# Attention loop of a two-layer decoder: copies moved between and ahead of exponentials, two sums moved ahead of pieces

## The chip, the cores and the metric

The program runs on one core of a Trainium2 chip. The time is the device time of one execution in microseconds (us). Five engines of the core work side by side, each through its own instructions in order, and wait for each other by semaphores: PE (TensorE, matmuls and transposes), ACT (ScalarE), DVE (VectorE), POOL (GpSimd) and SP, which here issues transfers. A matmul writes to `ps`, eight banks of PSUM of 128 x 512 words; only ACT, DVE and PE touch those here, so most results of PE have to be copied out by ACT or DVE before PE may use the bank again.

## The reference

Two decoder layers over x (2 x 512 x 128, that is 1,024 tokens) with a context of 2 x 77 rows. Each layer adds self attention, cross attention and a routed feed-forward block to x, each on a layer norm of x. The change lies in one loop, which holds the second layer's self attention, and beside it the first part of its cross attention:

```python
def _L1_attn_ref(x, w_q, w_k, w_v, w_o):          # 16 heads of 64
    scores = jnp.einsum('bhsq,bhtq->bhst', q, k)
    masked = jnp.where(causal, -jnp.inf, scores)
    weights = jax.nn.softmax(masked / jnp.sqrt(jnp.float32(dq)), axis=-1)
    out = jnp.einsum('bhst,bhtv->bhsv', weights, v)
    ...
    return jnp.einsum('bsf,df->bsd', cat, w_o)

def _L1_xattn_ref(x, knowledge_embeddings, ...):  # 16 heads of 8, 77 keys
    scores = jnp.einsum('bhsd,bhnd->bhsn', Q, K) / SCALE
    topk_scores, topk_indices = jax.lax.top_k(scores, 32)
    sparse_weights = jax.nn.softmax(topk_scores, axis=-1)
    context = jnp.einsum('bhsk,bhskd->bhsd', sparse_weights, sel_V)
    return context @ Wo.T + bo
```

The 32 largest of 77 scores are found on DVE in four rounds of eight: `max` gives the eight largest of a row, `match_replace` strikes them out.

## The kernel before

**Units.** The self attention is cut by pairs of heads (8) and by stages of 256 queries (4), which gives 32 values of j. A j is one unit U where the queries see few keys (stages 0 and 2: one unit holds a block of 128 keys and one of 256), or two units (stages 1 and 3: 384 keys, then 512). There are 48 units: 0 to 7 are stage 0, 8 to 23 stage 1, 24 to 31 stage 2, 32 to 47 stage 3. `FIRST[j]` is the first unit of j, `STAGE[k]` the first of a stage.

**What one unit goes through.** PE makes the scores (`scores(U)`, two heads, with the causal mask as a matmul), DVE takes the row maxima (`row_max`, L1164), ACT the exponentials with their sums (`exps`, L1608: two instructions for each block, one for each head, so four in a unit of two blocks), DVE the reciprocals (`row_inv`, L1170), POOL multiplies (`divide`, L712), PE turns the weights (`turn`, L2274), ACT copies the turned weights out (`evac_pt`, L1621, tile `prT`), and PE sums the values (`values(j)`, matmuls on `prT`) into bank 6. `evac_cat(j)` (L1616, the 128 x 256 copies into `sel_mem`, where `catT` lies) copies that sum out. Bank 6 is shared: before PE may project the values of the next heads (`project_v`, matmuls on `wT_hi` and `xt_hi`) or sum the next j, that copy has to be done (`cat_ready`).

**The loop.** `for U in range(NU)` stands once for each engine, and its body's order is the engine's order. In step U, PE does scores(U + 2), projects queries and keys (`project_qk`, bank 4) or values for a later j, turns U, and sums the j that ended with unit U - 1 (the sum stands ahead of the turn in the units of `VALUES_FIRST`). The second half of `turn(U)` writes bank 4 and so waits until ACT has copied the newly projected queries and keys (`evac_qk`, L1592). ACT in step U copies out what is due (`evac_cat`, `evac_qk`, `evac_v`), then `evac_pt(U)`, then `exps(U + 2)`, then the rest. DVE does `row_max(U + 2)`, `row_inv(U + 1)`, and a piece of the cross attention.

**Pieces.** From unit 12 to 46 the loop carries pieces (n, r): group n of four heads, round r of the four rounds of eight. One round is `eight` and `remove` on DVE (L1209 and L1219, eight instructions each, the latter with eight short loads). From n = 4 on, a unit with r = 2 does rounds 2 and 3. POOL follows with `shift`, `gone` and `pick`; PE turns the picked weights of n in two halves (`weights_x`, L2336), ACT copies each half out (`weights_T`, L1669, 77 x 512 into `sel_mem`), PE multiplies by the values (16 matmuls of nine columns, `context`), ACT copies that (`evac_cx`, L1663). All of these use bank 7 in turn, and PE's list `seven` holds what has to be done with the bank before it is written again.

**Ends of stages.** When a stage's heads are summed, PE projects them (`project_out`), DVE adds the product to x and takes the statistics of the next norm (`add_attention`), POOL makes the inverse deviation (`rstd_two`, L720, and the offset, L722), ACT applies the norm (`apply_two`, L1635), PE turns the result (`norm_two`, L2310). The same follows the cross attention of stages 0 and 1: at unit 36 and 44 (`OUT`) DVE normalises the context (`context_norm`, L1235), PE turns and projects it (`project_context`, matmuls on `w_x1T` and `cnT`), and in the next unit DVE adds it to x (`add_context`, L1244), after which come the statistics (L1174 to L1181). The projected context lies in bank 6, and PE waits for that sum to x before the next `values`.

Of the kernel before, what the change touches and what calls it, by code (L numbers as in the profile page):

```python
# [17 lines left out]
B, S, D, P = 2, 512, 128, 128  # L18
# [5 lines left out]
NP = H // 2  # L24
# [9 lines left out]
FIRST, UNIT, STAGE = [], [], []  # L34
# [9 lines left out]
NU = len(UNIT)  # L44
STAGE.append(NU)
FIRST.append(NU)
OUT = (36, 44)
# [15 lines left out]
def piece_of(U):  # L63

    if 12 <= U < 28:
        return divmod(U - 12, 4)
    if 29 <= U < 47:
        return 4 + (U - 29) // 3, (U - 29) % 3
    return None, None


NS = 2 * TB + E - 1
BIG = 4096.0

# [36 lines left out]
def decoder(nc, x_in, ctx_in, a0_wq, a0_bq, a0_wk, a0_bk, a0_wv, a0_bv, x0_wq, x0_bq, x0_wk, x0_bk, x0_wv,  # L111
# [5 lines left out]
    with ExitStack() as held:  # L117
# [732 lines left out]
        def _(dve):  # L850
# [375 lines left out]
            def context_norm(k):  # L1226

                dve.wait_ge(cx_ready, 4 * (k + 1))
                all_of = cx[:, k % 2, :, :].rearrange("p n (t h d) -> p n t h d", t=2, h=4)
                dve.reciprocal(cinv[:, :, :].rearrange("p n a -> p (n a)"),  # L1230
                               cx[:, k % 2, :, :].rearrange("p n (a d) -> p (n a) d", d=DX + 1)[:, :, DX])\
                   .then_inc(dve_step, own.up())
                dve.wait_ge(dve_step, own.now())
                for t in range(2):
                    dve.tensor_tensor(cn[:, t, :].rearrange("p (n h d) -> p n h d", h=4, d=DX),  # L1235
                                      all_of[:, :, t, :, 0:DX],
                                      cinv[:, :, 4 * t:4 * t + 4].unsqueeze(3).to_broadcast([P, 4, 4, DX]),
                                      ALU.mult).then_inc(cn_ready, 1)

            def add_context(k, source):  # L1240
                dve.wait_ge(xo_ps, k + 1)
                dve.wait_ge(bias_added, k + 1)
                t = slice(2 * k, 2 * k + 2)
                dve.tensor_tensor(x[:, t, :], x[:, t, :], source.rearrange("p (t d) -> p t d", t=2), ALU.add)\  # L1244
                   .then_inc(xo_used, 1)
                dve.wait_ge(xo_used, k + 1)
                stats_two(k, gn_var)

# [3 lines left out]
            for U in range(NU):  # L1252
                n, r = piece_of(U)
                if U + 2 < NU:
                    row_max(U + 2)
                if U + 1 < NU - 1:
                    row_inv(U + 1)
                for k in range(2):
                    if U == OUT[k]:
                        context_norm(k)  # L1260
                if r is not None:
                    eight(n, r)
                    remove(n, r)
                if double_step(U):
                    eight(n, 3)
                    remove(n, 3)
                if U == 0:
                    apply_first(1)
                if U == 2:
                    norm_stats(7)  # L1270
                if U == 3:
                    norm_apply(7, 9)
                for k in range(3):
                    if U == STAGE[k + 1] + 1:
                        add_attention(k, ps[:, (6, 7, 6)[k], 0:2 * P])
                if U == NU - 3:
                    row_inv(NU - 1)
                for k in range(2):
                    if U == OUT[k] + 1:
                        add_context(k, ps[:, 6, 0:2 * P])  # L1280


            def gates(i, first, n, bank):
# [135 lines left out]
            for j in range(NS):  # L1419
                gate(j)  # L1420
                if j == 4:
                    context_norm(2)
                if j == 6:
                    add_context(2, ps[:, 4, 0:2 * P])
                if j == 11:
                    gates(1, 4, 2, 4)
                if j == 13:
                    shares_of(1, 4, 2)
                if j == 14:
                    chosen_of(1, 4, 2)  # L1430
                cross(E + j)
            for i in range(4 * E):
                gate(NS + i)
                if i % 2 == 0 and i:
                    combine(i // 2 - 1)
                if i == 5:
                    context_norm(3)
                if i == 7:
                    add_context(3, ps[:, 4, 0:2 * P])
                if i == 12:  # L1440
                    gates(2, 6, 2, 4)
                if i == 14:
                    shares_of(2, 6, 2)
                if i == 15:
                    chosen_of(2, 6, 2)
                if i in (14, 15):
                    add_sparse(i - 14)
                cross(E + NS + i)
# [4 lines left out]
        def _(act):  # L1453
# [144 lines left out]
                act.activation(v_all[:, 2 * h:2 * h + 2, g:g + 2, :].rearrange("p t g n -> p t (g n)"),  # L1598
                               ps[:, bank, :].rearrange("p (t n) -> p t n", t=2), ACT.Copy).then_inc(v_ready, 1)

            def exps(U):
                s = U % 2
                act.wait_ge(nmax_ready, through(U))
                if U >= 3:
                    act.wait_ge(pt_ps, U - 2)
                for c, at, i in UNIT[U][1]:
                    for h in range(2):
                        act.activation(pr[U % 3][:, h, at:at + (c + 1) * P], ps[:, 2 * s + h, at:at + (c + 1) * P],  # L1608
                                       ACT.Exp, bias=nmax[:, i % 8, h:h + 1], accum_out=rsum[:, i % 8, h:h + 1])\
                           .then_inc(ex_ready, 1)  # L1610
# [21 lines left out]
            def apply_two(k, rstd_done, ready):  # L1632
                act.wait_ge(rstd_done, k + 1)
                for t in (2 * k, 2 * k + 1):
                    act.activation(xn[:, t, :], x[:, t, :], ACT.Identity, bias=offset[:, t:t + 1], scale=rstd[:, t:t + 1])\  # L1635
                       .then_inc(ready, 1)
# [49 lines left out]
            for U in range(NU):  # L1686
                n, r = piece_of(U)
                spare = ps[:, 7, 0:2 * P]
                for j in range(4 * NP - 1):
                    if U == FIRST[j + 1] + 1:  # L1690
                        evac_cat(j)
                for j in range(3, 4 * NP):
                    if U == FIRST[j] - 3:
                        evac_qk(j, 4)
                        if j in (NP + 2, 2 * NP + 2):
                            tokens_high(j // NP + 1)
                for j in range(2, 4 * NP, 2):
                    if U == FIRST[j] - 1:
                        evac_v(j, 6)
                for k in range(3):  # L1700
                    if U == STAGE[k + 1] + 3:
                        evac_qc(k, spare)
                if U == 12:
                    scores(0, 1, 7)
                if U == 13:
                    scores(1, 1, 7)
                if U == 28:
                    scores(4, 0, 7)
                if r == 0 and n + 1 in EARLY:
                    scores(n + 1, 0, 7)  # L1710
                if r == 2 and n >= 1:
                    weights_T(n - 1, 1, 7)
                evac_pt(U)
                if U == NU - 3:
                    weights_T(n - 1, 0, 7)
                if U + 2 < NU:
                    exps(U + 2)
                for k in range(3):
                    if U == STAGE[k + 1] + 2:
                        apply_two(k, qn_rstd, qn_ready)  # L1720
                for k in range(2):
                    if U == OUT[k] + 2:
                        apply_two(k, gn_rstd, gn_ready)
                if U == 1:
                    tokens_both(1, 8, spare)
                if U == 4:
                    norm_T(7, 9)
                if U == 11:
                    scores(0, 0, 7)
                if U == 12:  # L1730
                    scores(1, 0, 7)
                if U == 28:
                    scores(4, 1, 7)
                if r == 0 and n + 1 in EARLY:
                    scores(n + 1, 1, 7)
                if r == 1 and n >= 1 and U != NU - 3:
                    weights_T(n - 1, 0, 7)
                if r == 2 and n >= 1:
                    evac_cx(n - 1, 7)
                if r == 2:  # L1740
                    weights_x(n)
                for k in range(3):
                    if U == STAGE[k + 1] + 2:
                        norm_two(k, qnT_ps, qnT_ready, spare)
                for k in range(2):
                    if U == OUT[k]:
                        evac_cn(k, spare)
                    if U == OUT[k] + 3:
                        norm_two(k, gnT_ps, gnT_ready, ps[:, 6, 0:2 * P])
# [985 lines left out]
```

## Time and profile before

| What | Value |
|---|---|
| median of 3 runs (lowest to highest) | 580.23 us (576.71 to 580.39) |
| the profiled execution: its time, its span | 578.94 us, 577.1 us |
| busy, share of the span: PE, DVE, ACT, POOL | 89%, 67%, 54%, 39% |
| the chain that ended last, by engine | PE 58%, DVE 19%, ACT 11%, issue 5%, POOL 5% |
| mean granted clock of TensorE | 0.991 |

The loop fills the span from about 132 us (the scores of unit 0) to 388 us. The median is 0.2% over the profiled execution's time, and sums below are made against 578.94 us. In rows of the trace a time stands first (us from the span's start), then how long the instruction or a run of like instructions took; what stands in brackets is how long the engine was idle just before, and who ended that. Matmuls and transposes are pipelined, so those of a run overlap.

### The profile page before, as it was taken

To read this page: it belongs to the slowest core of one execution; us is meant where nothing else is said; L and a number is where in the kernel's file an instruction comes from. 1 tells how busy PE (TensorE), PEld (TensorE's weight loads), DVE (VectorE), ACT (ScalarE), POOL (GpSimd) and SP (SyncE) were. 2 spreads that over 40 slices of the span, in tenths; PEclk is the share of its full clock that TensorE was granted. 3 is DMA by queue.
4 is the path that set the end of the run, shared out by engine and by line. 5 is a ranking of instruction groups with operands and counts; after the bars stand their busy time and mean duration, and the time that the engine had idled before them with its cause. 6 is when DMAs were issued, how large, how long until landed. Compare 5 with 4: busy or idle time off the path is not lost.

```text
span 577.1 us, 12108 instructions
## 1 busy us (share of the span) xinstructions
PE 513.5 (89%) x3929; PEld 408.6 (71%) x3929; DVE 387.7 (67%) x2194; ACT 311.0 (54%) x779; POOL 224.8 (39%) x236
## 2 busy tenths in 40 slices
PE   4888779998998999988999889988889899899997
PEld 2566347866766677767677657677668779799997
DVE  3576775634422697775498799988968889544633
ACT  2343325436786677674875557657765464232221
POOL 5014950004434464562554556634832443340000
PEclk9999999999999999999999999999899999999999
DMA  4700105704000000000000000005400000010000
GB/s 117 214 1 15 46 25 148 205 15 165 2 0 1 2 2 2 1 2 1 2 2 2 1 2 1 2 2 165 136 26 20 15 15 20 10 33 2 28 1 10
DMA packets 24089, 21.04 MB, mean 36 GB/s; under 512 B 2175, under 2 KB 18643, under 8 KB 24027
## 3 DMA queue, kind: packets, MB, share of 16 engines
q1 hardware_dynamic: 23515, 19.21, 11.2%
q0 software_dynamic: 512, 1.05, 0.6%
q8 instruction: 33, 0.54, 0.4%
q14 instruction: 29, 0.24, 0.1%
HBM read 17.22 MB, written 3.03 MB: 35 GB/s over the span
## 4 chain that ended last, share of the span: by engine, by line
PE 58%; DVE 19%; ACT 11%; issue 5%; POOL 5%; DMA 1%; DVEq 0%; ACTq 0%; POOLq 0%
PE ps L1880 48%; PE ps L2274 5%; DVE wk L1219 3%; ACT w_mem L1608 3%; DVE top L1209 2%; DVE sel_mem L1026 2%; PE ps L2336 2%; ACT f_mem L1570 2%; DVE sel_mem L1338 1%; DVE nmax L1164 1%; POOL xs_dram L802 1%; POOL wk L743 1%; ACT pr L1608 1%; PE ps L2551 1%; DVE bn L857 1%
## 5 line engine op out<-in xcount | busy, mean ns | idle before, releaser
L1164 DVE TENSOR_REDUCE nmax<-ps 128x2 f32<-128x256 f32 (+1 forms) x64 | 51.1, 820 | 59.5 <-PE ps L1880 57.2
L1219 DVE MATCH_REPLACE8 wk<-top,wk 128x77 f32<-128x77 f32 x384 | 80.5, 223 | 0.0
L712 POOL TENSOR_TENSOR w_mem<-w_mem,rinv 128x256 f32<-128x256 f32 (+3 forms) x44 | 53.1, 1218 | 50.0 <-DVE rinv L1170 49.5
L1338 DVE TENSOR_TENSOR sel_mem<-gr,ps 128x512 f32<-128x512 f32 x47 | 32.2, 686 | 47.6 <-ACT gr L1816 46.9
L1816 ACT ACTIVATE gr<-ps 128x512 f32<-128x512 f32 x47 | 28.1, 598 | 57.3 <-PE ps L1880 57.3
L1209 DVE MAX8 top<-wk 128x8 f32<-128x77 f32 x384 | 57.9, 223 | 0.4
L1880 PE MATMUL ps<-cat_mem 64*128 64x256 f32 (+7 forms) x276 | 55.5, 473 | 1.5 <-ACT cat_mem L1592 1.5
L743 POOL TENSOR_SCALAR wk<-wk 128x616 f32<-128x616 f32 x16 | 28.1, 1754 | 65.5 <-DVEq L1223 65.2
L1621 ACT ACTIVATE prT<-ps 128x768 f32<-128x768 f32 (+1 forms) x48 | 42.4, 884 | 20.6 <-PE ps L2274 20.2
L1608 ACT ACTIVATE w_mem<-ps,nmax 128x128 f32<-128x128 f32 (+3 forms) x88 | 44.5, 522 | 3.4 <-DVE nmax L1164 3.3
L1880 PE MATMUL ps<-prT,cat_mem 128*64 128x128 f32 x640 | 42.0, 277 | 4.1 <-DVE x L1244 2.5
L1880 PEld LDWEIGHTS ps<-prT,cat_mem 128*64 128x64 f32 x640 | 34.4, 136 | 10.2 <-issue 4.7
L1880 PE MATMUL ps<-fd,sel_mem 128*128 128x128 f32 x256 | 34.7, 278 | 4.1 <-DVE sel_mem L1338 3.1
L712 POOL TENSOR_TENSOR pr<-pr,rinv 128x768 f32<-128x768 f32 (+3 forms) x20 | 26.6, 1341 | 29.0 <-DVE rinv L1170 28.7
L1880 PEld LDWEIGHTS ps<-fd,sel_mem 128*128 128x128 f32 x256 | 31.2, 192 | 5.9 <-DVE sel_mem L1338 5.9
L1880 PE MATMUL ps<-x_hi,w_hi 128*128 128x256 f32 x128 | 34.5, 304 | 0.0
L1880 PE MATMUL ps<-x_hi,w_lo 128*128 128x256 f32 x128 | 31.9, 282 | 0.0
L1880 PEld LDWEIGHTS ps<-vh,sel_mem 77*128 77x128 f32 x256 | 29.8, 192 | 2.6 <-ACT sel_mem L1669 1.3
L1592 ACT ACTIVATE cat_mem<-ps 128x512 f32<-128x512 f32 x32 | 19.4, 606 | 21.6 <-PE ps L1880 21.4
L2274 PE MATMUL ps<-ident,w_mem 128*128 128x128 f32 x212 | 29.9, 276 | 1.3 <-ACT cat_mem L1592 0.9
L1880 PE MATMUL ps<-vh,sel_mem 77*128 77x9 f32 x256 | 30.6, 256 | 0.4 <-ACT sel_mem L1669 0.4
L1219 DVE MATCH_VALUE_LOAD wk<-top,wk 128x8 f32 x384 | 30.5, 79 | 0.0
(362 smaller groups left out, 1316.2 us busy)
## 6 DMA issues: line engine op xcount, KB each, us to landing
w_mem<-in_L_ffn_W_dram SPq DMA_DIRECT2D x12, 256.0 KB, 3.3
f_mem<-in_L_ffn_Wg_dram SPq DMA_DIRECT2D x8, 256.0 KB, 2.9
f_mem<-in_L_ffn_Wu_dram SPq DMA_DIRECT2D x8, 256.0 KB, 3.3
f_mem<-in_L_ffn_Wd_dram SPq DMA_DIRECT2D x8, 256.0 KB, 4.0
sel_mem<-slot_dram SPq DMA_DIRECT2D x7, 256.0 KB
sel_mem<-in_L_ffn_W_dram SPq DMA_DIRECT2D x4, 256.0 KB, 4.8
xs_dram<-zero SPq DMA_DIRECT2D x1, 960.0 KB, 6.3
ys_dram<-f_mem SPq DMA_DIRECT2D x15, 64.0 KB, 1.5
```

The lines of the kernel that those rows point to most:

```text
L712: pool.tensor_tensor(pr[s][:, :, at:at + n], pr[s][:, :, at:at + n], rinv[:, i % 8, :].unsqueeze(2).to_broadcast([P, 2, n]), ALU.mult)\
L743: pool.tensor_scalar(wk[q][:, :, :, :], wk[q][:, :, :, :], NEG, None, ALU.is_le)\
L1164: dve.tensor_reduce(nmax[:, i % 8, :], ps[:, 2 * s:2 * s + 2, at:at + (c + 1) * P], X, ALU.max, negate=True).then_inc(nmax_ready, 1)
L1209: dve.max(top[q][:, t, h, 8 * r:8 * r + 8], src[:, t, h, :]).then_inc(top_step, 1)
L1219: dve.match_replace(wk[q][:, t, h, :], top[q][:, t, h, 8 * r:8 * r + 8], src[:, t, h, :], GONE).then_inc(top_step, 1)
L1338: dve.tensor_tensor(hg[s][:, :], gr[s][:, :], ps[:, 2 * s + 1, :], ALU.mult)\
L1592: act.activation(qk_place(j), ps[:, bank, :].rearrange("p (w n) -> p w n", w=2), ACT.Copy)\
L1608: act.activation(pr[U % 3][:, h, at:at + (c + 1) * P], ps[:, 2 * s + h, at:at + (c + 1) * P], ACT.Exp, bias=nmax[:, i % 8, h:h + 1], accum ...
L1621: act.activation(prT[U % 3][:, :, 0:n], ps[:, 4:6, 0:n], ACT.Copy).then_inc(ptc_ready, 1)
L1816: act.activation(gr[j % 2][:, :], ps[:, 2 * (j % 2), :], ACT.Relu).then_inc(gr_ready, 1)
L1880: return pe.matmul(dst, lhsT, rhs, start=start, stop=stop, skip_group_check=shared)
L2274: last = pe.transpose(tiles(4 + h)[:, k, :], pr[U % 3][:, h, k * P:(k + 1) * P], ident[:, :])
```

## The change

Nothing is computed otherwise, and no instruction is added or taken away; PE, POOL and SP keep their order. Four things move:

- **Copy of the summed heads** (ACT): for 11 of the 31 values of j (0 to 4, 14, 15 and 17 to 20), `evac_cat(j)` moves from the start of step `FIRST[j + 1] + 1` into step `FIRST[j + 1]`, between the exponentials of the first and of the second block of unit U + 2.
- **Copy of turned weights** (ACT): the first half's copy, `weights_T(n - 1, 0)`, moves ahead of `exps(U + 2)` at units 17, 21, 33 and 39. It already stood there at unit 45.
- **Norm** (ACT): at units 10, 26 and 34, `apply_two` moves ahead of `exps(U + 2)`.
- **Sum of the context to x** (DVE): at units 37 and 45 the sum is split from its statistics and moves ahead of the unit's piece; the statistics stay where they were.

```diff
+CAT_BETWEEN = tuple(j for j in range(4 * NP - 1) if (j % NP or not j) and FIRST[j + 1] + 2 < NU and len(UNIT[FIRST[j + 1] + 2][1]) == 2)
+TURNED_FIRST = tuple(U for U in range(NU) if piece_of(U)[1] == 1 and piece_of(U)[0] >= 1
+                     and (U not in FIRST or U in VALUES_FIRST))
...
+            def context_stats(k):
                 dve.wait_ge(xo_used, k + 1)
                 stats_two(k, gn_var)
...
+                for k in range(2):
+                    if U == OUT[k] + 1:
+                        add_context(k, ps[:, 6, 0:2 * P])
                 if r is not None:
                     eight(n, r)
                     remove(n, r)
...
                 for k in range(2):
                     if U == OUT[k] + 1:
-                        add_context(k, ps[:, 6, 0:2 * P])
+                        context_stats(k)
...
-            def exps(U):
+            def exps(U, between=None):
...
                 for c, at, i in UNIT[U][1]:
+                    if at and between is not None:
+                        evac_cat(between)
                     for h in range(2):
...
-                    if U == FIRST[j + 1] + 1:
+                    if U == FIRST[j + 1] + 1 and j not in CAT_BETWEEN:
                         evac_cat(j)
...
                 evac_pt(U)
-                if U == NU - 3:
+                if U in TURNED_FIRST:
                     weights_T(n - 1, 0, 7)
-                if U + 2 < NU:
-                    exps(U + 2)
                 for k in range(3):
                     if U == STAGE[k + 1] + 2:
                         apply_two(k, qn_rstd, qn_ready)
+                if U + 2 < NU:
+                    exps(U + 2, FIRST.index(U) - 1 if U in FIRST and FIRST.index(U) - 1 in CAT_BETWEEN else None)
...
-                if r == 1 and n >= 1 and U != NU - 3:
+                if r == 1 and n >= 1 and U not in TURNED_FIRST:
                     weights_T(n - 1, 0, 7)
```

**ACT, step 2 and the start of step 3** (stage 0; `prT` is evac_pt, `w_mem,rsum` the exponentials of unit 4, `sel_mem` the copy of the summed heads, the two `cat_mem` rows evac_qk and evac_v). Before:

```order
L1621 ACTIVATE prT<-ps 128x2x384
L1608 ACTIVATE w_mem,rsum<-ps,nmax 128x128 x2
L1608 ACTIVATE w_mem,rsum<-ps,nmax 128x256 x2
L1616 ACTIVATE sel_mem<-ps 128x256
L1592 ACTIVATE cat_mem<-ps 128x2x256
L1598 ACTIVATE cat_mem<-ps 128x2x256
```

Now:

```order
L1633 ACTIVATE prT<-ps 128x2x384
L1620 ACTIVATE w_mem,rsum<-ps,nmax 128x128 x2
L1628 ACTIVATE sel_mem<-ps 128x256
L1620 ACTIVATE w_mem,rsum<-ps,nmax 128x256 x2
L1602 ACTIVATE cat_mem<-ps 128x2x256
L1608 ACTIVATE cat_mem<-ps 128x2x256
```

The copy has moved ahead of the two longer exponentials; the two copies behind it are where they were.

**DVE, step 37** (`nmax` is row_max(39), `rinv` row_inv(38), MAX and MATCH_REPLACE the rounds 2 and 3 of piece 6, `x<-x,ps` the sum of the context, the rows from BN_STATS on the statistics). Before:

```order
L1164 TENSOR_REDUCE nmax<-ps 128x2
L1170 RECIPROCAL rinv<-rsum 128x2
L1209 MAX top<-wk 128x8 x8
L1219 MATCH_REPLACE wk<-top,wk 128x77 x8
L1209 MAX top<-wk 128x8 x8
L1219 MATCH_REPLACE wk<-top,wk 128x77 x8
L1224 ISA
L1244 TENSOR_TENSOR x<-x,ps 128x256
L1174 BN_STATS bn<-x 128x6 x2
```

Now:

```order
L1167 TENSOR_REDUCE nmax<-ps 128x2
L1173 RECIPROCAL rinv<-rsum 128x2
L1247 TENSOR_TENSOR x<-x,ps 128x256
L1212 MAX top<-wk 128x8 x8
L1222 MATCH_REPLACE wk<-top,wk 128x77 x8
L1212 MAX top<-wk 128x8 x8
L1222 MATCH_REPLACE wk<-top,wk 128x77 x8
L1227 ISA
L1177 BN_STATS bn<-x 128x6 x2
```

The sum has moved ahead of both rounds, and with it DVE's wait for PE's projection.

## Rows read from the trace of the kernel before

**Rows 1.** DVE's waits in the loop: who, for whom, us in total, times, longest.

```profile
DVE nmax L1164 <- PE ps L1880: 53.2, 23, 4.1
```

**Rows 2.** Stretches of DVE: length, busy us (instructions), TensorE's granted clock, DMA share, GB/s.

```profile
209.00:245.00 36.00, 28.91 (x194) 1.00 0.00 1
340.00:375.40 35.40, 33.54 (x233) 1.00 0.01 2
```

**Rows 3.** PE's waits in the loop.

```profile
PE ps L1880 <- ACT sel_mem L1616: 4.3, 7, 0.9
PE ps L1880 <- DVE x L1244: 2.5, 2, 1.8
```

**Rows 4.** Timeline, ACT, then PE: start, us, instruction, [idle before it].

```profile
151.75 0.40 ACT L1616 ACTIVATE sel_mem<-ps 128x256 f32<-128x256 f32 x1
152.02 0.63 ACT L1592 ACTIVATE cat_mem<-ps 128x512 f32<-128x512 f32 x1
152.21 0.39 PE L1880 MATMUL ps<-wT_hi,xt_hi 128*128 128x256 f32 x1 [0.90 <-ACT sel_mem L1616]
153.03 0.82 PE L2274 MATMUL ps<-ident,w_mem 128*128 128x128 f32 x6
343.62 0.39 PE L1880 MATMUL ps<-wT_hi,xt_hi 128*128 128x256 f32 x1 [0.29 <-ACT sel_mem L1616]
```

**Rows 5.** Timeline of POOL, ACT, PE around unit 10.

```profile
183.37 0.20 POOL L722 TENSOR_TENSOR offset<-minus_mean,rstd 128x2 f32<-128x2 f32 x1
184.72 0.87 ACT L1635 ACTIVATE xn<-x,offset,rstd 128x128 f32<-128x128 f32 x2
185.74 0.41 PE L2310 MATMUL ps<-ident,xn 128*128 128x128 f32 x2 [1.41 <-ACT xn L1635]
```

**Rows 6.** Timeline of PE at units 18, 22 and 26.

```profile
218.61 0.66 PE L2336 MATMUL ps<-ident,ex_mem 128*77 128x128 f32 x4 [1.43 <-ACT sel_mem L1669]
238.12 0.66 PE L2336 MATMUL ps<-ident,ex_mem 128*77 128x128 f32 x4 [0.60 <-ACT sel_mem L1669]
269.77 0.44 PE L2310 MATMUL ps<-ident,xn 128*128 128x128 f32 x2 [1.71 <-ACT sel_mem L1663]
```

**Rows 7.** Timeline of DVE, PE, POOL, units 37 to 39.

```profile
332.34 0.15 DVE L1170 RECIPROCAL rinv<-rsum 128x2 f32<-128x2 f32 x1
338.35 0.42 DVE L1244 TENSOR_TENSOR x<-x,ps 128x256 f32<-128x256 f32 x1 [0.31 <-DVE wk L1219]
334.07 0.69 PE L1880 MATMUL ps<-w_x1T,cnT 128*128 128x128 f32 x4
344.86 1.09 PE L2274 MATMUL ps<-ident,w_mem 128*128 128x128 f32 x8 [0.26 <-POOL w_mem L712]
339.98 0.73 POOL L720 TENSOR_TENSOR rstd<-var_eps,minus_half 128x2 f32<-128x2 f32 x1 [5.95 <-DVEq L1183]
342.91 1.90 POOL L712 TENSOR_TENSOR w_mem<-w_mem,rinv 128x1024 f32<-128x1024 f32 x1
```

**Rows 8.** Timeline of PE, DVE, POOL, ACT, units 45 and 46.

```profile
376.54 0.61 PE L1880 MATMUL ps<-w_x1T,cnT 128*128 128x128 f32 x4
376.57 0.16 DVE L1170 RECIPROCAL rinv<-rsum 128x2 f32<-128x2 f32 x1
379.41 0.16 DVE L1170 RECIPROCAL rinv<-rsum 128x2 f32<-128x2 f32 x1
379.65 1.90 POOL L712 TENSOR_TENSOR pr<-pr,rinv 128x1024 f32<-128x1024 f32 x1 [0.19 <-DVE rinv L1170]
382.81 0.88 ACT L1635 ACTIVATE xn<-x,offset,rstd 128x128 f32<-128x128 f32 x2 [2.48 <-POOL offset L722]
```

**Rows 9.** Busy us of PE by stretch, columns as in rows 2.

```profile
267.50:270.00 2.50, 0.79 (x8) 1.00 0.00 0
270.00:275.00 5.00, 5.00 (x30) 0.66 0.00 0
337.50:340.00 2.50, 1.17 (x22) 1.00 0.00 0
```

More of the change, by code:

```diff
@@ L1424, in _ @@
                     add_context(2, ps[:, 4, 0:2 * P])
+                    context_stats(2)
                 if j == 11:
@@ L1439, in _ @@
                     add_context(3, ps[:, 4, 0:2 * P])
+                    context_stats(3)
                 if i == 12:
```

## The prediction

> **What bounds the kernel now.** I read the chain of waits of the whole span first: PE holds 58% of it, and ACT and DVE come in only where PE waits for a copy or a sum. So the loop is paced by PE, in its own order, and a change is worth the PE waits that it takes away, less those that it makes. Then the totals of waits in the loop: PE idles 4.3 us, seven times, for the copy of the summed heads, and 2.5 us, twice, for the sum of the context to x [rows 3]. DVE waits 23 times for PE's scores, 53.2 us in all [rows 1]. The reader should see there that DVE has room, but not everywhere: from 209 to 245 us (stage 1) it is busy for 28.91 of 36 us, from 340 to 375.4 us (stage 3) for 33.54 of 35.4 [rows 2]. In stage 3 DVE is as full as PE. A microsecond taken from PE counts before that; a microsecond of waiting given to DVE counts in it. Last, the timelines at the places that move.
>
> **The copies between exponentials.** In step 2 the copy starts at 151.75 and lets PE project values at 152.21, after 0.90 us of idling [rows 4]. Now it starts before the two longer exponentials, about 0.9 us sooner, as PE is ready for it, so the wait goes. What is late next is ACT's copy of the queries and keys: it has the same work ahead of it as before, still starts at 152.02 and ends at 152.65 [rows 4]. The transposes that began at 153.03 could now begin at 152.13; their first half can, the second half waits for that copy, so they end about 0.7 us sooner, not 0.9. Of the 4.3 us, 0.29 belong to step 39 [rows 4], whose copy is not moved: 4.0 are left. Three of the places are of the 0.9 us kind, and each keeps back 0.2 to 0.3 us: 0.7. I take **3.3 us** off. Bounds: 4.0 if nothing is late next, 2.0 if half of it comes back as such waits. Five of the eleven copies stand where PE did not wait; they give nothing.
>
> The price: the second block's exponentials come 0.27 us later (the copy's share of ACT, 151.75 to 152.02 [rows 4]). What follows them is DVE's reciprocal, POOL's product and the turn two units on; DVE idles 2.3 us on average at each of its 23 waits [rows 1], and that covers it. Without that cover it would cost at most 11 times 0.27, 3 us. ACT does not wait in the middle for the sum: where that stands ahead of the turn it is long done, and elsewhere it runs beside the copy of the turned weights and the first exponentials.
>
> **The norm ahead of exponentials.** At unit 10 PE idles 1.41 us for it. POOL's offset is there at 183.57, the norm starts at 184.72 [rows 5], so it can start 1.15 us sooner: **1.2 us** off (between 0 and 1.4). The exponentials behind it move by the norm's 0.87 us, and only a turn two units on needs them. At unit 26 PE's wait, 1.71 us, is for the copy of the context (L1663), not for the norm [rows 6]; that copy has norm and exponentials ahead of it in either order, and now the copy of the heads too: **0.3 us** on. At unit 34 PE waits for the context's matmuls, and nothing changes.
>
> **The turned weights ahead of exponentials.** Units 17 and 21: PE waits 1.43 and 0.60 us for that copy [rows 6], which now comes before 1.3 us of exponentials: **2.0 us** off, nothing later on PE being near (DVE has 7 of 36 us free there [rows 2]). At unit 33 PE has 32 matmuls to do meanwhile. At unit 39 DVE is full [rows 2], and PE would only wait later: nothing. The sum of what is won: 3.3 + 1.2 - 0.3 + 2.0 = 6.2 us.
>
> **The two sums ahead of pieces.** This is where I expect a loss. In step 37 DVE is through with its reciprocal at 332.49 and now wants the sum. PE's projection of the context begins at 334.07 and ends at 334.76 [rows 7]. Both times hang on the same event, the normalised context that DVE handed to PE, so upstream gains do not bring them closer. DVE therefore stands still for **2.3 us**, and behind it in its queue stand two rounds of the piece, the statistics, and the maxima for the next exponentials. Before, it filled that time with the rounds and reached the sum at 338.35, when the projection was long there [rows 7]. The statistics then come 2.3 us later; on them hang POOL's deviation (339.98), and behind it in POOL's queue the product at 342.91, for which PE's turn at 344.86 already waits 0.26 us [rows 7]. So all of the 2.3 us reaches PE, and the 1.8 us that PE no longer waits for the sum [rows 3] is only spent waiting for that turn. DVE has no room to catch up by 375 us [rows 2]. Bounds: 0, if PE had room that I don't see, to 2.6 with the handover.
>
> In step 45 the projection ends at 377.15, DVE is ready at 376.73 [rows 8]: a wait of 0.4 us. But the sum itself, some 0.42 us [rows 7], now also stands ahead of the piece and of the reciprocal at 379.41, which starts POOL's product (1.90 us from 379.65). POOL's deviation comes after that product, and ACT's norm at 382.81 waits for it, 2.48 us already [rows 8]. With the handover that is **1.0 us** on (between 0.4 and 1.3), on the chain that ends the loop.
>
> **Sum.** -6.2 + 2.3 + 1.0 = -2.9 us. The clock is left. After PE's idle time around 268 us (0.79 us busy in 2.5) the granted clock is 0.66 over the next 5 us, partly at the lower of its two levels, 1.2 instead of 2.4 GHz: 1.7 us lost. Yet after 1.17 busy in 2.5 at 337.5 nothing falls [rows 9]. PE's freed time ahead of the turn of unit 39 and POOL's delay make about 4.3 us of idle time there (1.8 + 0.3 + 2.3). One fall costs between 0 and 1.7 us, as DVE and not PE alone paces that stretch [rows 2]; I take 0.8, the middle. 578.94 - 2.9 + 0.8 = **576.8 us**, 0.6% under the median shown, which is itself 0.2% over the profiled execution.
>
> [...]
>
> **The rivals.**
> 1. *The sums cost nothing* (15%). DVE's wait would be hidden, if PE's projection came before DVE's reciprocal. Then only the gains stand: 578.94 - 6.2 = 572.7, and down to 570 if PE's 2.5 us of waits for the sum come back too. For it: PE does wait there. Against it: 334.76 stands after 332.49.
> 2. *The clock falls at both gaps* (17%): ahead of the turn of unit 39, and ahead of the norm after unit 46, where PE, with its 0.7 us share of the waits for the sum gone, stands idle until ACT's norm. Each costs the full 1.7 us: 578.94 - 2.9 + 3.4 = 579.4, slower than before, and about 581 with a third. It decides from the second fall on, since one (1.7) is less than the 2.9 won. For it: the fall after 268 us. Against it: 337.5.
> 3. *The gains do not arrive* (10%): the queries' and keys' copy, or DVE, takes over each wait. Half of 6.2 gives 578.94 - 3.1 + 3.3 = 579.1; none gives 582.2.
>
> My forecast has the remaining 58%, with 574.5 to 579 as its own range (gains of 4.9 to 7.4, falls of 0 to 1.7). The range that should hold 8 in 10 runs from 571.5, most of rival 1, to 581.5, most of 2 and 3. A measurement of this kernel tells about 1% from no change, so faster means under 574.4 and slower over 586.0, against the median. Faster: rival 1 and the lower edge of the forecast, 0.24. Slower: 0.05. Same: 0.71.
>
> **What would show it.** Right: PE's waits for L1616 fall from 4.3 us to under 1; those of 1.43 and 0.60 us for L1669 and 1.41 us for the norm go; DVE waits about 2.3 us for PE ahead of the first L1247 and 0.4 ahead of the second; PE waits some 4 us in pieces before the turn of unit 39; the stretch to unit 32 is about 6 us shorter, that from 32 to the end about 3 to 4 longer. Wrong: no such wait of DVE (rival 1), a granted clock under 0.9 around units 39 or 47 (rival 2), or new PE waits for L1602 as large as those gone (rival 3).

## The result and the profile after

The changed kernel took **585.97 us**, the median of 4 runs (581.79 to 587.81), against 580.06 for the kernel before, timed beside it: a ratio of 1.0112 (95% interval 1.0079 to 1.0145). 576.8 was predicted, and 581.5 was the upper end of the range. Timed again later (below), the ratio was 1.0026 (0.9988 to 1.0065). Ratios leave out runs some 1.5% or more above the fastest of their kernel, of the changed kernel one of 588.01 and one of 2,736.9 us in the later sample. So the change brings nothing, and costs up to 1%. The order of the engines came out within a microsecond or so of the forecast at each place. TensorE's clock did not.

The profiled execution took 581.79 us, with a span of 580.1 and a mean granted clock of 0.974 (before: 578.94, 577.1, 0.991). It is 2.85 us behind the profiled execution of before. Where that arises is read at one instruction that every unit has, ACT's copy of the turned weights. First the timeline of ACT after, then before, for units 0, 37, 38, 46 and 47 (start, us, instruction, idle before it):

```profile
142.14 0.81 ACT L1633 ACTIVATE prT<-ps 128x768 f32<-128x768 f32 x1 [0.64 <-PE ps L2286]
326.97 1.02 ACT L1633 ACTIVATE prT<-ps 128x1024 f32<-128x1024 f32 x1 [0.27 <-PE ps L2286]
335.80 0.81 ACT L1633 ACTIVATE prT<-ps 128x768 f32<-128x768 f32 x1
376.89 0.82 ACT L1633 ACTIVATE prT<-ps 128x768 f32<-128x768 f32 x1
382.85 1.02 ACT L1633 ACTIVATE prT<-ps 128x1024 f32<-128x1024 f32 x1
```

```profile
140.81 0.81 ACT L1621 ACTIVATE prT<-ps 128x768 f32<-128x768 f32 x1 [0.64 <-PE ps L2274]
332.42 1.02 ACT L1621 ACTIVATE prT<-ps 128x1024 f32<-128x1024 f32 x1 [0.27 <-PE ps L2274]
338.50 0.81 ACT L1621 ACTIVATE prT<-ps 128x768 f32<-128x768 f32 x1
379.51 0.82 ACT L1621 ACTIVATE prT<-ps 128x768 f32<-128x768 f32 x1
384.61 1.03 ACT L1621 ACTIVATE prT<-ps 128x1024 f32<-128x1024 f32 x1
```

The loop begins 1.33 us late. Twelve matmuls well before it took 5.16 us, at a granted clock of 0.5, where they took 2.75 before, and the change does not touch that place. PE after, and then before:

```profile
80.19 5.16 PE L1892 MATMUL ps<-later,ident 128*128 128x512 bf16 x12
```

```profile
80.78 2.75 PE L1880 MATMUL ps<-later,ident 128*128 128x512 bf16 x12
```

By unit 37 the changed kernel is 5.45 us ahead, so the loop has won **6.8 us**. By unit 38 it is 2.70 ahead: **2.75 us** given back behind the first sum, while the clock is still 1.00. By unit 46 it is 2.62 ahead, by unit 47 1.76: **0.86 us** behind the second sum. Yet it ends 3.0 us behind, so about 5 us are lost after the loop's last copy, where the change moves nothing.

PE's waits in the loop (who, for whom, us in total, times, longest) answer to [rows 3] and to the waits of [rows 5, 6]:

```profile
PE ps L2322 <- ACT sel_mem L1675: 2.3, 2, 2.0
PE ps L2322 <- ACT sel_mem L1628: 2.0, 1, 2.0
PE ps L1892 <- ACT sel_mem L1628: 1.6, 1, 1.6
PE ps L2322 <- ACT xn L1647: 0.3, 1, 0.3
```

L1628 is the copy of the summed heads: instead of seven waits of at most 0.9 us [rows 3] two are left, 1.6 and 2.0 us, both at new places. The norm of unit 10 makes PE wait 0.3 instead of 1.41 us [rows 5]. The waits of 1.43 and 0.60 us for the turned weights at units 18 and 22 [rows 6] are not there any more. Unit 26 waits 2.0 instead of 1.71 us, as predicted.

The first sum (L1247), in the timelines of DVE, ACT, POOL and PE, against [rows 7]:

```profile
329.35 0.42 DVE L1247 TENSOR_TENSOR x<-x,ps 128x256 f32<-128x256 f32 x1 [2.31 <-PE ps L1892]
335.48 0.43 ACT L1660 ACTIVATE sc<-ps 128x308 f32<-128x308 f32 x1 [5.42 <-issue]
335.95 0.79 PE L1892 MATMUL ps<-kh,qc 128*128 128x308 f32 x2 [2.67 <-ACT sc L1660]
336.74 0.73 POOL L723 TENSOR_TENSOR rstd<-var_eps,minus_half 128x2 f32<-128x2 f32 x1 [8.16 <-DVEq L1186]
340.38 0.38 PE L1892 MATMUL ps<-wT_hi,xt_hi 128*128 128x256 f32 x1 [1.60 <-ACT sel_mem L1628]
341.62 1.97 PE L2286 MATMUL ps<-ident,w_mem 128*128 128x128 f32 x8 [0.15 <-POOL w_mem L715]
```

DVE stands still for 2.31 us, where 2.3 were predicted. PE then waits 2.67 + 1.60 + 0.15 = 4.4 us in three pieces before the turn of unit 39; about 4.3 were predicted. The turn itself takes 1.97 instead of 1.09 us [rows 7]: a first fall of the clock, from about 341 to 344.5 us. It comes after unit 38's copy (335.80), so the 2.75 us are not its doing.

The second sum, after, and then before:

```profile
374.57 0.42 DVE L1247 TENSOR_TENSOR x<-x,ps 128x256 f32<-128x256 f32 x1 [0.47 <-PE ps L1892]
377.93 1.89 POOL L715 TENSOR_TENSOR pr<-pr,rinv 128x1024 f32<-128x1024 f32 x1 [1.09 <-DVE rinv L1173]
381.08 0.88 ACT L1647 ACTIVATE xn<-x,offset,rstd 128x128 f32<-128x128 f32 x2 [3.38 <-POOL offset L725]
382.58 0.37 ACT L1628 ACTIVATE sel_mem<-ps 128x256 f32<-128x256 f32 x1
383.05 0.66 PE L2322 MATMUL ps<-ident,xn 128*128 128x128 f32 x2 [1.98 <-ACT sel_mem L1628]
384.19 3.26 PE L1892 MATMUL ps<-prT,cat_mem 128*64 128x128 f32 x28 [0.48 <-ACT xnT L1637]
390.56 6.20 PE L1892 MATMUL ps<-woT,sel_mem 128*128 128x128 f32 x32
```

```profile
379.94 1.75 PE L1880 MATMUL ps<-prT,cat_mem 128*64 128x128 f32 x28 [0.74 <-DVE x L1244]
384.82 0.41 PE L2310 MATMUL ps<-ident,xn 128*128 128x128 f32 x2 [0.32 <-issue]
385.96 1.75 PE L1880 MATMUL ps<-prT,cat_mem 128*64 128x128 f32 x28 [0.73 <-ACT xnT L1625]
389.67 3.74 PE L1880 MATMUL ps<-woT,sel_mem 128*128 128x128 f32 x32
```

Before, PE waited 0.74 us for the sum and reached the turn of the norm as ACT was through with it. Now PE no longer waits for the sum and comes early, while POOL's deviation and with it ACT's norm, and the copy of the summed heads that ACT does behind it, come late for PE. PE stands idle 1.98 us ahead of the norm's turn. From there the same matmuls take nearly twice as long: 3.26 for 1.75 us, 6.20 for 3.74. The norm's turn still starts 1.77 us earlier than before, and `project_out` (`woT`) ends at 396.76 instead of 393.41, 3.35 later: this stretch alone cost **5.1 us**. The windows of PE show why (length, busy us, granted clock, DMA share, GB/s):

```profile
340.00:345.00 5.00, 4.46 (x22) 0.66 0.01 2
380.00:385.00 5.00, 2.53 (x20) 0.71 0.01 2
385.00:390.00 5.00, 4.47 (x34) 0.50 0.02 3
390.00:395.00 5.00, 5.00 (x25) 0.50 0.43 157
395.00:400.00 5.00, 4.86 (x36) 0.93 0.03 9
```

0.50 is the lower of the two levels, 1.2 GHz. The clock stays there from about 382, in PE's idle time, until about 396, some 13 us, though PE is busy for all of 390 to 395. Before, it was 1.00 in all of these stretches.

### The profile page after: what moved, and what is told of

It is laid out like the page before. It is cut to its first block, busy times and chain, and to the rows that moved or that the text cites. A ratio compares the mean times of both kernels' runs of the same rounds, so it can differ in the third digit from the quotient of the medians.

```text
span 580.1 us, 12108 instructions
## 1 busy us (share of the span) xinstructions
PE 520.1 (90%) x3929; PEld 413.9 (71%) x3929; DVE 387.7 (67%) x2194; ACT 309.7 (53%) x779; POOL 224.8 (39%) x236
## 3 DMA queue, kind: packets, MB, share of 16 engines
q0 software_dynamic: 512, 1.05, 0.6%
## 4 chain that ended last, share of the span: by engine, by line
PE 60%; DVE 18%; ACT 10%; POOL 6%; issue 5%; DMA 1%; DVEq 0%; ACTq 0%; POOLq 0%
PE ps L1892 50%; PE ps L2286 5%; DVE wk L1222 3%; DVE top L1212 2%; ACT w_mem L1620 2%; PE ps L2348 2%; DVE sel_mem L1029 2%; ACT f_mem L1580 2%; POOL wk L746 1%; DVE sel_mem L1346 1%; POOL xs_dram L805 1%; PE ps L2563 1%; POOL w_mem L715 1%; DVE bn L860 1%; ACT cat_mem L1602 1%
## 5 line engine op out<-in xcount | busy, mean ns | idle before, releaser
L1892 PE MATMUL ps<-prT,cat_mem 128*64 128x128 f32 x640 | 43.5, 284 | 0.6 <-ACT xnT L1637 0.5
L1892 PEld LDWEIGHTS ps<-prT,cat_mem 128*64 128x64 f32 x640 | 35.7, 140 | 6.5 <-issue 3.8
L2286 PE MATMUL ps<-ident,w_mem 128*128 128x128 f32 x212 | 31.2, 282 | 1.8 <-ACT cat_mem L1602 0.9
```

The source lines that it names most:

```text
L1892: return pe.matmul(dst, lhsT, rhs, start=start, stop=stop, skip_group_check=shared)
L2286: last = pe.transpose(tiles(4 + h)[:, k, :], pr[U % 3][:, h, k * P:(k + 1) * P], ident[:, :])
```

## Experiments

All times are medians of all runs, all ratios are against the kernel before, timed beside the run. What is won or lost is read from the ratios.

**The changed kernel again**, unedited, ten runs.

> The changed kernel once more, for a second trace beside the runs of this chip. Clock theory: the fall after unit 47 stands in this trace too, at about 380 to 396 us, and the ratio is 1.008 to 1.014. Rival (the four runs so far fell badly by chance): no such fall, ratio about 0.995.

581.33 us, ratio 1.0026 (0.9988 to 1.0065). The fall stands in this trace too, as expected (an execution of 588.01 us at a clock of 0.965): PE idles 1.99 us ahead of the norm's turn, and `project_out` is slow.

```profile
396.34 6.18 PE L1892 MATMUL ps<-woT,sel_mem 128*128 128x128 f32 x32
```

The ratio is under what was expected, and the intervals of the two samples do not meet. The clock goes with it: the median granted clock of the runs was 0.965 in the first sample (four runs) and 0.973 in the second (eight), and 0.985 for 69 runs of the kernel before. So "slower" is shown by the first sample alone. What both show is that a gain of 0.5%, which the engines' order gives, is not there.

**The two sums alone.** The kernel before, with the sum split and moved ahead of the piece, and nothing else.

```diff
...
+                for k in range(2):
+                    if U == OUT[k] + 1:
+                        add_context(k, ps[:, 6, 0:2 * P])
                 if r is not None:
...
-                        add_context(k, ps[:, 6, 0:2 * P])
+                        context_stats(k)
```

> The kernel before with nothing but the two sums ahead of their pieces. Clock theory: 2.7 and 0.9 us of waiting, 5 us of low clock after unit 47, maybe 1 to 2 around unit 39: ratio 1.014 to 1.018. Rival (the fall needs the shortened loop): 3.6 us alone, ratio 1.006.

586.27 us, 1.0116 (1.008 to 1.0151), a little under the theory's 1.014, with a median clock of 0.971. This part of the change alone loses 6.7 us by the ratio (1.16% of 578.81), twice the 3.3 of its order. In the one execution that was traced (590.12 us at a clock of 0.962) the fall is there without the shortened loop, but it is shorter:

```profile
392.87 0.66 PE L2317 MATMUL ps<-ident,xn 128*128 128x128 f32 x2 [1.99 <-ACT sel_mem L1623]
399.29 3.74 PE L1887 MATMUL ps<-woT,sel_mem 128*128 128x128 f32 x32
```

The gap is the same, but the clock is back at 398 us, and `project_out` runs at full speed. From the start of the norm's turn to its end 10.2 us pass, where the kernel before takes 8.6 and the changed one 13.7: this fall cost 1.6 us and not 5.1. The loop of this execution also begins 3.9 us later than that of the kernel before, ahead of anything that the edit moves.

**The copies alone.** The kernel before, with the eleven copies between exponentials.

```diff
...
+                    if at and between is not None:
+                        evac_cat(between)
...
-                    if U == FIRST[j + 1] + 1:
+                    if U == FIRST[j + 1] + 1 and j not in CAT_BETWEEN:
...
```

> The kernel before with nothing but the 11 copies between the exponentials. By the sum of the prediction 3.3 us of the gain are theirs (the trace of the change has 3.5 at units 1 to 6, 24 and 29, and loses 0.3 at unit 27): ratio 0.994 to 0.995. Rival (the clock decides, not the copies): anything from 0.99 to 1.00 with falls at other places.

575.29 us, 0.9925 (0.9894 to 0.9957): 4.3 us won by the ratio (0.75% of 578.81), 3.5 by the medians; 3.3 predicted.

**The change without its sums**, that is copies, norms and weights.

```diff
-                for k in range(2):
-                    if U == OUT[k] + 1:
-                        add_context(k, ps[:, 6, 0:2 * P])
...
+                        if k in (0, 1):
+                            add_context(k, ps[:, 6, 0:2 * P])
                         context_stats(k)
```

> The change without the two sums: copies, weights and norm stay ahead of exponentials, both sums of the context stand after the pieces again. Clock theory (the order of the engines wins 6.8 us by unit 37, the two sums give 3.6 back, and the rest of the loss is TensorE at its lower level for some 16 us after unit 47, brought on by PE's longer idle time ahead of the last norm): the gain stays, no fall of the clock after unit 47, 6 to 7 us under the kernel before, ratio 0.988 to 0.990. Rival (any shorter loop lets the clock fall after unit 47): the fall is there all the same, ratio 0.997 to 1.003.

574.46 us, 0.9895 (0.9845 to 0.9945): 6.1 us won by the ratio (1.05% of 579.16), 4.7 by the medians; 6.2 predicted. PE at the end of its loop:

```profile
379.65 0.41 PE L2321 MATMUL ps<-ident,xn 128*128 128x128 f32 x2 [0.32 <-issue]
384.50 3.74 PE L1891 MATMUL ps<-woT,sel_mem 128*128 128x128 f32 x32
```

PE idles no longer ahead of the norm's turn than before the change (0.32 us), and `project_out` takes 3.74 us.

**One sum at a time.** The changed kernel, with only the sum of unit 37 moved (first), or only that of unit 45 (second).

```diff
-                for k in range(2):
+                for k in (0,):
                     if U == OUT[k] + 1:
...
+                        if k in (1,):
+                            add_context(k, ps[:, 6, 0:2 * P])
```

> The change with only the first sum (unit 37) ahead of its pieces. Clock theory: the 2.3 us wait of DVE costs 2.7 us as in the changed kernel, no long fall after unit 47, so 4 us under before, ratio 0.993. Rival (the sums' waits are the whole loss): half of the loss comes back, ratio 1.000 to 1.005.

> The change with only the second sum (unit 45) ahead of its piece. Clock theory: this one alone makes PE idle 2.0 us ahead of the last norm, the clock stays low to about 396 us as in the changed kernel: 6.8 won, 0.9 and about 5 lost, ratio 0.997 to 1.000. Rival (the sums' waits are the whole loss): only 0.4 us of waiting, ratio 0.990.

First: 578.93 us, 0.9977 (0.9938 to 1.0016), more than the 0.993 expected. In its trace the first sum costs what it costs in the changed kernel: the copies of units 37 and 38 stand 2.76 us further apart than before (326.76 and 335.60 us). What made up the rest is open. Second: 579.21, 1.0008 (0.998 to 1.0035), just over the 0.997 to 1.000 expected. Against 0.9895 without sums, the second costs 1.1% although only about 1 us of order is at stake in it. Windows of PE with the first sum alone:

```profile
335.00:340.00 5.00, 4.25 (x14) 0.66 0.00 2
380.00:385.00 5.00, 3.42 (x42) 1.00 0.01 2
385.00:390.00 5.00, 5.00 (x49) 1.00 0.45 129
```

and PE with the second sum alone:

```profile
380.35 0.66 PE L2324 MATMUL ps<-ident,xn 128*128 128x128 f32 x2 [1.99 <-ACT sel_mem L1630]
387.86 6.01 PE L1894 MATMUL ps<-woT,sel_mem 128*128 128x128 f32 x32
```

Each fall belongs to its own sum. The one at unit 39 comes with the first, the one at unit 47 with the second, and in none of the twelve traces of this case is either there without it.

**The gap filled.** The changed kernel, with eight matmuls whose result nobody uses (`keep_busy`, which the program has for such a use elsewhere) in PE's idle time ahead of the last norm. They write to a bank that is free once the last exponentials have been read, and PE waits for those.

```diff
                     if U == OUT[k] + 3:
+                        if U == NU - 1:
+                            pe.wait_ge(ex_ready, 2 * through(NU - 1))
+                            keep_busy(3, 8)
                         norm_two(k, gn_ready, gnT_ps, gnT_ready, ...)
```

> The changed kernel with eight matmuls of 512 columns into a free bank in PE's idle time ahead of the last norm (step 47), which nobody reads. Clock theory: granted clock stays 1.00 from 380 to 396 us and about 5 us come back: ratio 0.993 to 0.996. Rival (the later norm itself is the loss): as the changed kernel, ratio 1.011.

575.88 us, 0.9916 (0.9883 to 0.9948): better than the theory's 0.993, and far from the rival's 1.011. PE:

```profile
382.11 1.89 PE L1892 MATMUL ps<-later,ident 128*128 128x512 bf16 x8
384.26 0.41 PE L2322 MATMUL ps<-ident,xn 128*128 128x128 f32 x2 [0.27 <-issue]
389.11 3.74 PE L1892 MATMUL ps<-woT,sel_mem 128*128 128x128 f32 x32
```

This removes no wait of any other engine; it only gives PE something to do in the gap. The norm's turn begins 0.10 us after ACT's copy of the summed heads has ended, as without filler. `project_out` is back at 3.74 us, and from the start of the norm's turn to its end 8.6 us pass instead of 13.7. That is the 5.1 us. The first sum's fall is still in its trace, at unit 39.

**The sums alone, with the same filler.** If DVE's waits were the loss, and the clock only a sign of them, filler would not help here.

> The kernel before with the two sums ahead of pieces alone, and eight matmuls of filler ahead of the norm of step 47 (the sums alone took 1.0116 of the kernel before). Theory (half of that loss is the clock's fall behind the second sum): no fall between 375 and 400 us, project_out in 3.8 us, ratio 1.001 to 1.007, the sums' own 3.3 us and a fall at unit 39 being left. Rival (the loss is DVE's waits and what they do to the pieces, and the clock is only a sign of it): 1.009 to 1.014.

581.61 us, 1.0044 (1.0015 to 1.0074), where the sums alone took 1.0116: as the theory said, and the two intervals do not meet. In its trace the clock is 1.00 from 375 to 400 us, and from the norm's turn to the end of `project_out` 8.6 us pass, where the trace of the sums alone has 10.2. By the ratios the filler gives back some 4 us, more than the 1.6 that this one trace of the sums alone shows for the fall. What is left, 2.6 us, is of the size of the sums' own cost in order (3.3 predicted).

**Filler where the kernel before falls too.** At about 270 us the clock fell before the change [rows 9], behind PE's wait for the context's copy [rows 6]. The change without its sums, with seven such matmuls ahead of the norm of step 26; then the same kernel again.

```diff
+                        if k == 1:
+                            pe.wait_ge(ex_ready, 2 * through(U + 1))
+                            keep_busy(3, 7)
                         seven = norm_two(k, qn_ready, qnT_ps, qnT_ready, spare, *seven)
```

> The change without the sums, and seven matmuls of 512 columns in PE's idle time at unit 26, ahead of the turn of the norm, where the clock falls at 265 us in every trace so far. Clock theory: that fall goes, 1.5 us on top of the version without the sums: ratio 0.986 to 0.988. Rival (the fall comes from what stands after it): ratio as without the filler, 0.9895.

> The change without its two sums and with seven matmuls ahead of the norm of step 26, timed again with more rounds. Theory (fewer falls of the clock, and the won 6 us kept): ratio 0.985 to 0.990 of the kernel before, granted clock 0.98 or more, clock 1.00 between 260 and 275 us. Rival (its first ratio was a lucky draw of falls elsewhere): 0.990 to 0.996.

571.46 us, 0.9866 (0.978 to 0.9953), and 572.03 us, 0.9857 (0.9809 to 0.9905). PE without the filler, and with it (first of the two):

```profile
265.47 0.44 PE L2321 MATMUL ps<-ident,xn 128*128 128x128 f32 x2 [1.98 <-ACT sel_mem L1674]
...
267.50:270.00 2.50, 2.50 (x12) 0.51 0.00 0
```

```profile
261.82 1.67 PE L1891 MATMUL ps<-later,ident 128*128 128x512 bf16 x7
263.94 0.44 PE L2321 MATMUL ps<-ident,xn 128*128 128x128 f32 x2 [0.45 <-ACT sel_mem L1674]
...
267.50:270.00 2.50, 2.47 (x29) 1.00 0.00 0
```

The fall is gone. This version, 1.4% faster than the kernel before, is the best found. By the ratios it is 0.3 to 0.4% better than without the filler (0.9895), but the intervals overlap.

**All runs at one clock.** Each run's time has its granted clock beside it. A straight line through those runs of a kernel that the ratios use gives its time at a clock of 0.979 (with two standard errors). It is rough, since a fall costs more at one place than at another: the slopes go from 0.17 to 0.51 us for 0.001 of clock.

| Kernel | runs | ratio | median clock | at 0.979, us | against before | predicted, order alone |
|---|---|---|---|---|---|---|
| before | 69 | 1 | 0.985 | 581.9 ± 0.4 | | |
| changed | 12 | 1.0112; 1.0026 | 0.965; 0.973 | 579.0 ± 1.8 | -2.9 | -2.9 |
| without sums | 7 | 0.9895 | 0.982 | 575.6 ± 0.8 | -6.3 | -6.2 |
| copies alone | 10 | 0.9925 | 0.987 | 577.6 ± 0.4 | -4.3 | -3.3 |
| sums alone | 10 | 1.0116 | 0.971 | 584.7 ± 1.7 | +2.8 | +3.3 |
| sums alone, filler | 12 | 1.0044 | 0.985 | 584.5 ± 0.8 | +2.6 | +3.3 |
| without sums, filler at unit 26 | 10 | 0.9866; 0.9857 | 0.985 | 575.7 ± 1.7 | -6.2 | -6.2 |
| first sum only | 9 | 0.9977 | 0.979 | 576.0 ± 1.1 | -5.9 | -3.9 |
| second sum only | 10 | 1.0008 | 0.976 | 578.4 ± 0.9 | -3.5 | -5.2 |
| changed, filler | 9 | 0.9916 | 0.985 | 577.6 ± 0.8 | -4.3 | -2.9 |

At equal clock the sum of the prediction holds within 1 us in the first six kernels, and misses by 1.4 to 2.0 us in the last three, so this table supports the account and does not prove it. What differs besides is the clock that each kernel gets: the sums take it from 0.985 to 0.971, and filler gives it back.

## Why the prediction was wrong

- **Copies, norms, weights:** -6.2 predicted, -6.8 between units 0 and 37 in the trace, -6.1 by the ratio of the runs without sums. Right, and so is what was said to stay (unit 26, 0.3 us on).
- **First sum:** +2.3 predicted, at most 2.6; 2.75 measured between units 37 and 38. DVE's wait was right (2.31 us). What was left out is that the sum's own 0.42 us now stands ahead of the piece too, a term that the prediction counted for the second sum only: DVE's last round ends at 335.33 us, before at 338.04, so 2.74 us of the 5.45 ahead are gone. The waits ahead of the turn of unit 39 were named in the right size (4.4 for 4.3 us). The path is partly another: the longest of them is not for POOL's product but for ACT's copy of scores (2.67 us), which starts 0.15 us after that last round.
- **Second sum:** +1.0 predicted, 0.86 between units 46 and 47 (ahead by 2.62 at unit 46, by 1.76 at 47).
- **The clock: this step failed.** "One fall costs between 0 and 1.7 us ... I take 0.8, the middle." The fall at unit 39, which the 0.8 was for, cost about 0.2: 2.70 us ahead at unit 38, 2.62 at unit 46, while the version without sums wins 0.14 over the same units. But the forecast counted only this fall, and no fall in the range cost more than 1.7 us. The second one, after unit 47, cost 5.1 us in this execution, three times the bound (by the same two rows 5.1 in the later trace of the changed kernel, 4.9 with the second sum alone, 1.6 with the sums alone). It was rival 2's place and its mechanism (PE without its share of the waits for the sum, idle until ACT's norm), and the sign named for it, a clock under 0.9 around units 39 or 47, is there at both. Rival 2 had a chance of 17%, and its price, 1.7, was taken from a fall in the middle of the loop. Two things were wrong in that. The fall lasts: some 13 us at 0.5 here, not 5 at a mean of 0.66 [rows 9]. And where it happens PE alone paces: behind the loop's end PE idles only 0.48 and 0.53 us between the norm's turn and the end of `project_out`, so what the clock takes comes through nearly whole. The prediction had this in hand. It said that the second sum's delay lies "on the chain that ends the loop", and priced the clock for a stretch where "DVE and not PE alone paces".
- With 5.1 us in that place and 0.2 for the first fall in place of the 0.8, the prediction's own sum gives 578.94 - 2.9 + 5.3 = 581.3, against 581.79 in the profiled execution. That it comes so near is partly luck: 1.33 us from the fall at 80 us, which nobody counted, and the 0.45 of the first sum stand against 0.6 more won in the loop and 0.35 that come back behind `project_out`. The median of that sample is 4 us above this execution.

Three things stay open. The other runs of the first sample are up to 6 us slower than the profiled one at clocks of 0.962 to 0.965; where their further falls lie no trace of them shows. In the trace of 588.01 us at 0.965 the loop begins 3.94 us later than before the change, so falls ahead of the loop may be part of it. Nor is it shown why the fall after unit 47 lasts some 13 us in three traces and 7 in that of the sums alone. And that the two samples differ (1.0112, 1.0026) is described by their clocks, not explained.

## What to carry to other kernels

Price an idle gap of PE by what stands behind it: where PE alone paces what follows, a gap of 2 us can cost 5 more through the clock (1.6 in another trace), and a gap in a stretch that another engine paces next to nothing (0.2). When a change takes away a wait in front of some matmuls and delays the step behind them, look where the two leave PE idle, and put the granted clock of the stretch after it into the sum. Matmuls of no use in such a gap cost PE nothing there; eight of them took the sums alone from 1.0116 to 1.0044 of the kernel before.

## What the runs showed of the hardware

The twelve matmuls at 80 us took 2.75 us in one execution and 5.16 in the other with the same work ahead of them. The kernel with filler at unit 26 was traced twice: at 485 to 490 us its clock was 0.52 in the first trace and 1.00 in the second, at 220 to 225 us it was 1.00 in the first and 0.67 in the second. So a fall can come or stay away from run to run, and the runs of one kernel spread by several us (584.19 to 590.18 for the sums alone, at clocks of 0.962 to 0.979).

Once fallen, the clock stayed at 0.50 through 390 to 395 us, where PE was busy for 5.00 of 5.00 us, and came back only at about 396. The Trainium skill, "TensorE: Matmul & The Clock Gate", "What's actually happening", says that activity releases the throttle. After the wait at 265 us the trace of the version without sums agrees: 0.51 over 267.5 to 270, 1.00 from 270. After unit 47 of the changed kernel the clock comes back only much later.

A small DVE instruction waits for POOL. In the statistics behind the second sum, two values per partition are written while POOL's product (377.93 to 379.82) runs, and that took 1.29 us; behind the first sum, with POOL idle, 0.17. Timeline of DVE after, and then before:

```profile
336.37 0.17 DVE L1183 TENSOR_SCALAR minus_mean<-mean_var 128x2 f32<-128x2 f32 x1
378.55 1.29 DVE L1183 TENSOR_SCALAR minus_mean<-mean_var 128x2 f32<-128x2 f32 x1
```

```profile
380.73 0.84 DVE L1180 TENSOR_SCALAR minus_mean<-mean_var 128x2 f32<-128x2 f32 x1
```

It ends at 379.84 (378.55 + 1.29), 0.02 us after the product. The Trainium skill, "SBUF — State Buffer", "Who interferes with whom", says that such a DVE instruction can need a pair of ports shared with POOL and then stands still until POOL's instruction has ended; the trace agrees. Before the change it took 0.84 us at this place and ended 0.02 us after the product too. The longer stand adds nothing to the 0.86 us of the second sum: ACT's norm starts 1.26 us after the end of POOL's product in both kernels. The 0.86 us arise ahead of the product, for which POOL now waits 1.09 instead of 0.19 us [rows 8], as DVE's reciprocal has the wait for the sum (0.47) and the sum (0.42) ahead of it.
